# Gated delta rule: a root moved to GpSimd, one more round of lag, and two units' block merging taken together

## The chip, the cores and the metric

The kernel runs on one core of one Trainium2 chip. Its time is the device time of one execution in microseconds (us). It has five queues that run side by side: TensorE (PE; PEld is its weight load), VectorE (DVE), ScalarE (ACT), GpSimd (POOL), and the sync queue (SP), which here issues every DMA. Each queue is strictly in order; the queues wait for one another with semaphores.

## The reference, cut to what matters

The reference is a decoder of four layers on 16 sequences of 128 tokens and width 256, that is eleven more stages behind the one that is changed. The change is in the first stage, the gated delta rule:

```python
q, k, v = (silu(causal_conv4(x @ W)) for W in (Wq, Wk, Wv))      # 16 heads of 128
alpha, beta = sigmoid(x @ Wa + ba), sigmoid(x @ Wb + bb)
for each token:  S = alpha * S - beta * (S k - v) k^T ;  o = S q
o = (o - mean) * rsqrt(var + 1e-5) * ln_g + ln_b
out = (o * sigmoid(x @ Wg)) @ Wo
```

The kernel does the token loop of one sequence in closed form: with N the strictly lower, decayed 128x128 matrix of beta k k^T, it needs the inverse of (1 + N), applied to v, and then a second masked matrix applied to that.

## The kernel before

`Delta` (lines 320 to 832) does 64 units, one head of four sequences each, tile 128x512. `order()` (L452) writes out by hand a software pipeline of rounds: round t does the first half of unit a = t (projections k and q, convolutions, decay), the score matrices of unit t-1, and the second half of units v = t-LAG, w = t-LAG-1 and x = t-LAG-2 (projections v and gate, the rest of the inverse, the products, the norm, the output). PE, ACT and DVE all follow this one list of steps. In it PE's line L310 is a projection, L502 the scores, L518 and L527 and L530 the merging of 32x32 blocks (steps x32 and y32), L537 and L543 that of 64x64 blocks (x64, y64), L557 step w, L564 step o, L571 the turned o, L580 the output (acc), L550 the turned v.

The inverse of (1 + N) is made in two parts. The 32x32 blocks on the diagonal are inverted by GpSimd, for a batch of up to eight units (128 blocks, one on each partition): a first instruction (L826) and then 30 dependent pairs (L830, L831), and a turned copy (L832). The blocks reach it through DRAM: SP writes each unit's N (L380), reads a batch into `NB` (L387), writes the inverses out (`blocks_out`, L399) and reads them back by unit into `T` and `TT` (`blocks_in`, L409 and L412, seven DMAs a unit). Then x32, y32, x64 and y64 join the blocks: each is a handful of small matmuls into PSUM bank 7 and a copy by ACT (L647, L653, L654, L657, L660), one waiting for the other.

SP's queue is written by `load()` (L344): in iteration t it loads two weights for the unit t+4 once PE has done q of unit t, three weights for the second half, `blocks_out` and `blocks_in` where due, and then the N of unit t-1. There is one buffer `NB`, so the load of batch m waits for the inversion of batch m-1 (L385).

The norm of o (step o) is DVE's: four statistics (L222), four aggregates (L225) and then eleven small instructions on 128x4 for the inverse root (L196 to L214: a shift, a subtraction, three Newton steps) and one for the mean (L784). ACT applies it (step on, L678, four instructions) and only then may PE write bank 4 again: `room[4] = self.on.at(u + 1)`, which step s0 waits for. The rows of a group of four sequences are normed in steps stats, scale and turn, in every 16th round.

Of the kernel before, what the change touches and what calls it, by code (L numbers as in the profile page):

```python
# [11 lines left out]
ALU = mybir.AluOpType  # L12
# [3 lines left out]
NB = 16  # L16
T = 128
# [48 lines left out]
class Core:  # L66
# [4 lines left out]
    def __init__(self, nc, ctx, ins, out):  # L71
# [12 lines left out]
        self.rsq = self.at("rsq", [128, 16], F32)  # L84
        self.free0 = self.low
# [60 lines left out]
    def start_vector(self, dve, own):  # L146
        dve.memset(self.ones[:, :], 1.0)
        dve.wait_ge(self.dma_const, 48)
        dve.tensor_copy(self.identb[:, :], self.ident[:, :])
        dve.tensor_copy(self.neg[:, :], self.negf[:, :]).then_inc(*self.const.up)  # L150
# [51 lines left out]
    def rsqrt_rest(self, dve, own, w):  # L202
# [12 lines left out]
        return o  # L215

# [103 lines left out]
class Delta(Stage):  # L320
# [6 lines left out]
    U, LAG, RING = 64, 12, 14  # L327
    BATCHES = (4, 4) + (8,) * 6 + (4, 4)

    def weights(self):  # L330
# [4 lines left out]
        self.id32 = c.f32("did", 32, 32)  # L335
# [8 lines left out]
    def load(self, sp):  # L344
# [9 lines left out]
        sp.dma_start(self.id32[:, :, :], i["c_ident"][0:32, 0:32].unsqueeze(0).broadcast_to([128, 32, 32])).then_inc(small, 16)  # L354
        for t in range(-4, self.U + self.LAG):
# [15 lines left out]
            if 0 <= v - 1 < self.U:  # L371
                self.blocks_in(sp, v - 1)
            if 0 <= n < self.U:
# [7 lines left out]
                if n == self.first[m] + self.BATCHES[m] - 1:  # L381
                    so_far = sum(self.BATCHES[i] for i in range(m % 2, m + 1, 2))
                    sp.wait_ge(self.n_sem[m % 2], 64 * so_far)
                    if m:
                        sp.wait_ge(*self.sub.at(m))  # L385
                    P = 16 * self.BATCHES[m]
                    sp.dma_start(self.NB[0:P, :, :], self.Nd[m % 2].rearrange("u b k s t -> (u b k) s t")[0:P]).then_inc(self.nb_sem[m % 2], 16)  # L387
# [14 lines left out]
    def blocks_in(self, sp, v):  # L402
# [4 lines left out]
        for k in range(4):  # L407
            of = self.TTd[m % 2, v - self.first[m], :, k, :, :].rearrange("b c t -> c b t")
            sp.dma_start(g4(self.TT[v % 4][blk(k, 32), :])[:, :, blk(k, 32)], of).then_inc(self.t_sem[v % 4], 16)  # L409
        for k in range(3):  # L410
            of = self.Td[m % 2, v - self.first[m], :, k, :, :].rearrange("b t c -> t b c")
            sp.dma_start(self.T[v % 4][blk(k, 32), :, blk(k % 2, 32)], of).then_inc(self.t_sem[v % 4], 16)  # L412

    def buffers(self):
# [13 lines left out]
        self.TT, self.T, self.X = c.sets(4, "dTT", 512), c.sets(4, "dT", 4, 64), c.sets(2, "dX", 4, 64)  # L428
        self.NB, self.TB, self.TTB, self.tmp = c.f32("dNB", 32, 32), c.f32("dTB", 32, 32), c.f32("dTTB", 32, 32), c.f32("dtmp", 256)
# [13 lines left out]
        self.sc, self.vt, self.x32, self.y32, self.x64, self.y64 = t("score", 2 * U), t("v_turned", U), t("x32", U), t("y32", U), t("x64", U), t("y64", U)  # L443
        self.wm, self.o, self.ot, self.accd = t("w", U), t("o", U), t("ot", U), t("acc", U)
        self.ck, self.cq, self.cv, self.hk, self.hq, self.hv = s("k0", U), s("q0", U), s("v0", U), s("k_tanh", U), s("q_tanh", U), s("v_tanh", U)
        self.vk, self.xc32, self.yc32, self.xc64, self.yc64 = s("v", U), s("x32", U), s("y32", U), s("x64", U), s("y64", U)
        self.wc, self.on, self.os, self.gt, self.ex = s("w", U), s("o", U), s("o_turned", U), s("gate", U), s("exp", U)
        self.dk, self.dq, self.dv, self.sk, self.sq, self.sv = v("k", U), v("q", U), v("v", U), v("k_silu", U), v("q_silu", U), v("v_silu", U)
        self.nr, self.rs, self.go, self.summed = v("scores", 2 * U), v("o", U), v("gated", U), v("summed", 4)
        self.sub = p("inverses", len(self.BATCHES))  # L450

    def order(self):  # L452


        for t in range(self.U + self.LAG + 5):
# [4 lines left out]
            for step, u in every:  # L460
                if 0 <= u < self.U and (step not in ("close", "stats", "scale", "turn") or u % 16 == 15) and (step, u) != ("turn", self.U - 1):
                    yield step, u, u % self.RING, u // 16, u % 16

    def tensor(self, pe):
        c, bank, room = self.c, self.c.bank, self.c.room
        pe.wait_ge(self.dma[0], 176)
# [16 lines left out]
        for step, u, r, g, h in self.order():  # L483
# [28 lines left out]
            elif step == "x32":  # L512
                pe.wait_ge(*room[7])
                pe.wait_ge(self.dma[11 + u % 4], 112 * (u // 4 + 1))
                for b in range(4):
                    for k in range(2):
                        lo, hi = blk(2 * k, 32), blk(2 * k + 1, 32)
                        t = pe.matmul(bank(7)[hi, blk(b, 32)], self.NT[r][lo, 128 * b + 64 * k + 32:128 * b + 64 * k + 64],  # L518
                                      self.T[u % 4][lo, b, 0:32], start=True, stop=True, tile_position=(64 * k, 64 * k + 32))
                t.then_inc(*self.x32.up)  # L520
            elif step == "y32":
                pe.wait_ge(*self.xc32.at(u + 1))
                TT = g4(self.TT[u % 4][:, :])
                for b in range(4):
                    for k in range(2):
                        lo, hi = blk(2 * k, 32), blk(2 * k + 1, 32)
                        pe.matmul(bank(7)[lo, 128 + 32 * b:160 + 32 * b], self.X[s][hi, b, 0:32], TT[hi, b, hi], start=True, stop=True,  # L527
                                  tile_position=(64 * k + 32, 64 * k))
                    lo, hi = blk(0, 32), blk(1, 32)
                    t = pe.matmul(bank(7)[hi, 256 + 32 * b:288 + 32 * b], TT[hi, b, hi], self.X[s][hi, b, 0:32], start=True, stop=True,  # L530
                                  tile_position=(32, 32))
                t.then_inc(*self.y32.up)
            elif step == "x64":
                pe.wait_ge(*self.yc32.at(u + 1))
                lo, hi = blk(0, 64), blk(1, 64)
                for b in range(4):
                    t = pe.matmul(bank(7)[hi, blk(b, 64)], self.NT[r][lo, 128 * b + 64:128 * b + 128], self.T[u % 4][lo, b, :], start=True, stop=True)  # L537
                t.then_inc(*self.x64.up)
            elif step == "y64":
                pe.wait_ge(*self.xc64.at(u + 1))  # L540
                lo, hi, TT = blk(0, 64), blk(1, 64), g4(self.TT[u % 4][:, :])
                for b in range(4):
                    t = pe.matmul(bank(7)[lo, 256 + 64 * b:320 + 64 * b], self.X[s][hi, b, :], TT[hi, b, hi], start=True, stop=True)  # L543
                t.then_inc(*self.y64.up)
                room[7] = self.yc64.at(u + 1)
# [3131 lines left out]
```

## Time and profile before

| what | value |
|---|---|
| median of 3 runs | 3936.02 us (3934.26 to 3938.75) |
| the profiled execution | 3935.08 us, of which its span 3933.3 us |
| PE, DVE, ACT, POOL busy, whole span | 86%, 76%, 49%, 29% |
| the Delta stage | from 0 to about 1180 us |
| its rounds with both halves, 178 to 995 us | PE busy 793.7 of 817.0 us, DVE 736.3, ACT 519.6, POOL 261.6; granted clock 1.00 |
| its start, 0 to 178 us | PE busy 122.7 us, clock 0.89 |
| its end, 995 to 1180 us | PE busy 161.2 of 185.0 us, clock 0.94 |

A line of the timeline gives start, duration (from the start of the first to the end of the last instruction of a run of equal ones), engine, line, operation, tiles written and read, shapes and count; in brackets the idle time of the engine before it and what ended it. Matmuls overlap, so the time that a group takes of PE is the distance to the start of the next group, not its duration.

### The profile page before, as it was taken

What the parts mean: (1) busy time and instruction counts of PE and PEld (TensorE: products, weight loads), DVE (VectorE), ACT (ScalarE), POOL (GpSimd) and SP (SyncE); (2) the same over time, 40 slices, a digit from 0 to 9 for tenths busy, and PEclk for the clock granted to TensorE, in tenths of its full rate; (3) what the DMA queues carried; (4) which work ended last, traced back from release to release, by engine and by line L of the source; (5) the groups of instructions that cost most, each with busy time, mean ns of one, the idle gap of its engine ahead of it and who ended that gap; (6) DMA issues with size and microseconds to landing.
All of it is one profiled execution on the core that took longest, in us unless ns stands there. A gap on an engine that the chain in (4) does not pass through costs nothing.

```text
span 3933.3 us, 63955 instructions
## 1 busy us (share of the span) xinstructions
PE 3367.4 (86%) x22787; PEld 2145.2 (55%) x22802; DVE 2988.6 (76%) x6462; ACT 1945.5 (49%) x4750; POOL 1135.5 (29%) x1162
## 2 busy tenths in 40 slices
PE   7799999999886295888999978889999999997775
PEld 3366666665554243664556655565655656564444
DVE  7799988989656866554367767768988898986668
ACT  4466666666553142331144425436656655563455
POOL 1533033206401200000011122015655555554110
PEclk9899999999998598898999989899999999998887
DMA  2222222222211000001000000302222222222000
GB/s 71 61 71 56 68 63 68 58 63 62 51 34 47 13 23 24 2 2 63 1 22 1 1 33 2 123 6 89 78 70 76 70 75 76 70 75 77 1 1 22
DMA packets 240233, 183.98 MB, mean 47 GB/s; under 512 B 117744, under 2 KB 216432, under 8 KB 239024
## 3 DMA queue, kind: packets, MB, share of 16 engines
q1 hardware_dynamic: 239920, 179.90, 15.5%
q8 instruction: 185, 3.03, 0.3%
q14 instruction: 128, 1.05, 0.1%
HBM read 164.61 MB, written 15.20 MB: 46 GB/s over the span
## 4 chain that ended last, share of the span: by engine, by line
PE 59%; DVE 28%; issue 5%; ACT 5%; POOL 2%; SPq 1%; DMA 1%; DVEq 0%; ACTq 0%; POOLq 0%
PE ps L310 21%; PE ps L3273 5%; PE ps L2908 4%; PE ps L3261 3%; PE ps L502 2%; PE ps L2953 2%; DVE hMX L3026 2%; PE ps L2695 1%; DVE macc L3413 1%; PE ps L580 1%; PE ps L1972 1%; PE ps L3252 1%; PE ps L2914 1%; PE ps L2171 1%; PE ps L316 1%
## 5 line engine op out<-in xcount | busy, mean ns | idle before, releaser
L310 PE MATMUL ps<-xT,min 128*128 128x512 f32 (+1 forms) x1072 | 499.3, 610 | 30.2 <-DVE macc L3413 29.8
L3413 DVE SCALAR_TENSOR_TENSOR macc<-ps,mcw,macc 128x508 f32<-128x508 f32 (+2 forms) x408 | 302.2, 741 | 77.8 <-ACT macc L3340 68.1
L3495 POOL TENSOR_TENSOR mSQ<-mSQ,mtn 128x512 f32<-128x512 f32 x128 | 243.1, 1900 | 353.3 <-ACT mtn L3365 353.3
L310 PEld LDWEIGHTS ps<-xT,min 128*128 128x128 f32 (+1 forms) x1072 | 190.8, 190 | 249.2 <-issue 202.9
L3488 POOL TENSOR_TENSOR mE<-mE,mCB 128x1024 f32<-128x1024 f32 x128 | 302.1, 2360 | 44.4 <-DVE mE L3423 26.3
L3423 DVE TENSOR_TENSOR_SCAN mE<-mE,mid 128x1024 f32<-128x1024 f32 x128 | 297.3, 2322 | 0.0
L3273 PE MATMUL ps<-mwo,macc 128*128 128x256 f32 x1024 | 243.1, 380 | 5.4 <-DVE macc L3430 5.3
L3026 DVE TENSOR_REDUCE hMX<-ps 128x2 f32<-128x512 f32 x256 | 165.4, 687 | 104.1 <-PE ps L2914 104.1
L3361 ACT ACTIVATE mtn<-ps,mcol 128x64 f32<-128x64 f32 x1024 | 222.9, 334 | 2.8 <-PE ps L3252 2.8
L826 POOL TENSOR_TENSOR dTB<-did,dNB 128x1024 f32<-128x1024 f32 (+1 forms) x10 | 29.1, 2908 | 664.1 <-DMA dNB<-d_N 598.7
L2993 ACT ACTIVATE hE<-ps 128x512 f32<-128x512 f32 x256 | 138.9, 594 | 153.0 <-PE ps L2908 153.0
L2914 PE MATMUL ps<-hKE,hXE 32*128 32x256 f32 x1024 | 170.5, 457 | 37.8 <-issue 15.1
L3273 PEld LDWEIGHTS ps<-mwo,macc 128*128 128x128 f32 x1024 | 184.7, 190 | 28.5 <-DVE macc L3430 8.5
L2908 PE MATMUL ps<-hXE,hKE 32*128 32x256 f32 x1024 | 156.6, 423 | 49.5 <-DVE hMX L3026 40.2
L2360 POOL TENSOR_TENSOR lP<-lP,lm 128x512 f32<-128x512 f32 x64 | 66.8, 1044 | 452.2 <-DVE lm L2333 452.2
L732 DVE SCALAR_TENSOR_TENSOR dav<-ps,dsmall,dav 128x508 f32<-128x508 f32 (+2 forms) x192 | 142.3, 741 | 47.0 <-ACT dav L603 42.5
L831 POOL TENSOR_TENSOR dTB<-dTB,dtmp 128x30 f32<-128x30 f32 (+11 forms) x300 | 169.6, 565 | 23.5
L732 DVE SCALAR_TENSOR_TENSOR daq<-ps,dsmall,daq 128x508 f32<-128x508 f32 (+2 forms) x192 | 142.5, 742 | 42.6 <-ACT daq L603 37.2
L732 DVE SCALAR_TENSOR_TENSOR dak<-ps,dsmall,dak 128x508 f32<-128x508 f32 (+2 forms) x192 | 142.2, 741 | 25.1 <-ACT dak L603 20.5
L830 POOL TENSOR_TENSOR dtmp<-dNB,dTB 128x30 f32<-128x30 f32 (+11 forms) x300 | 154.0, 513 | 23.5
L502 PE MATMUL ps<-dKQ 128*128 128x256 f32 x512 | 137.7, 396 | 24.6 <-ACT dO L678 17.0
L2264 ACT ACTIVATE lP<-ps,lm 128x128 f32<-128x128 f32 x256 | 90.6, 366 | 129.9 <-DVE lm L2327 129.9
(594 smaller groups left out, 8281.0 us busy)
## 6 DMA issues: line engine op xcount, KB each, us to landing
mE<-m_decay SPq DMA_DIRECT2D x128, 512.0 KB, 3.7
dwk<-in_L_attn_Wk SPq DMA_DIRECT2D x64, 128.0 KB, 2.3
dwq<-in_L_attn_Wq SPq DMA_DIRECT2D x64, 128.0 KB, 2.3
dwv<-in_L_attn_Wv SPq DMA_DIRECT2D x64, 128.0 KB, 2.4
dwg<-in_L_attn_Wg SPq DMA_DIRECT2D x64, 128.0 KB, 2.4
dwo<-in_L_attn_Wo SPq DMA_DIRECT2D x64, 128.0 KB, 2.7
min<-in_m_in SPq DMA_DIRECT2D x2, 4096.0 KB, 17.1
d_N<-dNT SPq DMA_DIRECT2D x256, 16.0 KB, 1.5
```

Of the source, the lines that this page charges most:

```text
L310: t = pe.matmul(out, w[:, j, :], self.c.xT[:, j, blk(g, 512)], start=j == 0, stop=j == 1)
L502: t = pe.matmul(bank(4 + i)[:, blk(j, 256)], self.KQ[s][:, 2 * i + j, 0, :], self.KQ[s][:, 2 * i + j, :, :], start=True, stop=True)
L732: x = dve.scalar_tensor_tensor(out=acc[:, :, 3 - j:T], in0=p[:, :, 0:T - 3 + j], scalar=small[:, 4 * k + j:4 * k + j + 1], in1=acc[:, :, 3 ...
L2908: m = pe.matmul(self.c.bank(n)[:, blk(h, 256)], self.KE[x][r, e, blk(h)], self.XE[x][r, e, :], start=True, stop=True)
L2914: m = pe.matmul(self.c.bank(n)[:, blk(1 - h, 256)], self.XE[t % 4][r, h, blk(e)], self.KE[t % 4][r, h, :], start=True, stop=True)
L3026: dve.tensor_reduce(self.MX[y][:, k // 2, r:r + 32:16], bank(n).rearrange("p (e n) -> p e n", e=2), AX.X, ALU.max, negate=True).then_inc(* ...
L3273: t = pe.matmul(bank(to + j // 2)[:, blk(j % 2, 256)], self.acc[s][:, blk(j)], self.wo[:, i, :], start=i == 0 and j % 2 == 0, stop=i == 31 ...
L3361: x = act.activation(self.tn[s][:, h], bank(6)[:, h], ACT.Copy, scale=self.col[:, 4 * g + j, 2 * i + e:2 * i + e + 1])
L3413: x = dve.scalar_tensor_tensor(out=acc[:, :, 3 - j:T], in0=p[:, :, 0:T - 3 + j], scalar=self.cw[:, i, j:j + 1], in1=acc[:, :, 3 - j:T], op ...
L3423: dve.tensor_tensor_scan(E, E, self.id8[:, :, :].rearrange("p b t -> p (b t)"), 0.0, ALU.mult, ALU.add).then_inc(*self.de.up)
L3488: pool.tensor_tensor(E, E, bc(self.CB[g % 2][:, :, :].rearrange("p b t -> p (b t)"), 2), ALU.mult).then_inc(*self.em.up)
L3495: pool.tensor_tensor(self.SQ[g % 2][:, :], self.SQ[g % 2][:, :], self.tn[s][:, :], ALU.add).then_inc(*self.sqa.up)
```

## The change

Five things are changed in the stage.

1. The inverse root and the negated mean of step o go to GpSimd: DVE stops after the four aggregates and signals, GpSimd does four instructions on 128x4 (a product by -1, an addition, a power of -0.5, a product). The group's root in step stats goes there too (two instructions).
2. GpSimd's inversion is cut into parts (three of ten pairs each; the last batch into four), placed in the same rounds as the roots: in round t GpSimd does first the root of unit w, then the part that is due.
3. LAG is 13 instead of 12, the ring of N and its companion has 15 instead of 14 places, and the batches are (4, 4) and seven of 8, where they were (4, 4), six of 8, (4, 4).
4. There are two buffers `NB`; the load of batch m waits for the inversion of batch m-2. The first instruction of an inversion no longer reads an identity `did` (its DMA is gone) but is a product by -1 and a memset of the diagonal.
5. The steps x32, y32, x64 and y64 are done in every second round, for units u and u+1 together; the number of matmuls is the same, the copies of ACT are half as many and twice as wide. `blocks_in` is issued for both units in one iteration of SP, every second iteration.

```diff
-    U, LAG, RING = 64, 12, 14
-    BATCHES = (4, 4) + (8,) * 6 + (4, 4)
+    U, LAG, RING = 64, 13, 15
+    BATCHES = (4, 4) + (8,) * 7
...
-        sp.dma_start(self.id32[:, :, :], i["c_ident"][0:32, 0:32].unsqueeze(0).broadcast_to([128, 32, 32])).then_inc(small, 16)
...
-            if 0 <= v - 1 < self.U:
+            if 0 <= v - 1 < self.U and v % 2:
                 self.blocks_in(sp, v - 1)
+                self.blocks_in(sp, v)
...
-                    if m:
-                        sp.wait_ge(*self.sub.at(m))
+                    if m >= 2:
+                        sp.wait_ge(*self.sub.at(m - 1))
...
+                if step in ("x32", "y32", "x64", "y64") and u % 2:
+                    continue
...
             elif step == "x32":
                 pe.wait_ge(*room[7])
-                pe.wait_ge(self.dma[11 + u % 4], 112 * (u // 4 + 1))
-                for b in range(4):
-                    for k in range(2):
+                T = self.T[u // 2 % 2]
+                for z in range(2):
+                    pe.wait_ge(self.dma[11 + (u + z) % 4], 112 * ((u + z) // 4 + 1))
+                    N = self.NT[(u + z) % self.RING]
+                    for b in range(4):
+                        for k in range(2):
...
             elif step == "o":
-                o = c.moments(dve, own, [(p[:, blk(j)], 0) for j in range(4)], st, sw, 1e-5 / 128)
+                for j in range(4):
+                    o = own(dve.bn_stats(st[:, j, 0:6], p[:, blk(j)]))
                 dve.wait_ge(own.sem, o)
-                dve.scalar_tensor_tensor(out=st[:, :, 0:1].rearrange("p a b -> p (a b)"), in0=st[:, :, 6:7].rearrange("p a b -> p (a b)"),
-                                         scalar=-1.0, in1=sw[:, 0:4], op0=ALU.mult, op1=ALU.mult).then_inc(*self.rs.up)
+                for j in range(4):
+                    x = dve.bn_aggr(st[:, j, 6:8], st[:, j, 0:6])
+                x.then_inc(*self.var.up)
...
     def gpsimd(self, pool, own):
+        for t in range(self.U + self.LAG + 5):
+            w, x = t - self.LAG - 1, t - self.LAG - 3
+            if 0 <= w < self.U:
+                st, sw = self.s8[w % 2], self.sw[w % 2]
+                pool.wait_ge(*self.var.at(w + 1))
+                pool.tensor_scalar(flat(st[:, :, 0:1]), flat(st[:, :, 6:7]), -1.0, 1.0, ALU.mult, ALU.mult)
+                then(c.root_pool(pool, own, sw[:, 0:4], flat(st[:, :, 7:8]), 1e-5 / 128, sw[:, 4:8]))
+                pool.tensor_tensor(flat(st[:, :, 0:1]), flat(st[:, :, 0:1]), sw[:, 0:4], ALU.mult).then_inc(*self.rs.up)
+            if 0 <= x < self.U and x % 16 == 15:
+                pool.wait_ge(*self.xvar.at(x // 16 + 1))
+                c.root_pool(pool, own, c.rsq[:, 0:4], flat(c.st[:, :, 7:8]), 1e-5, c.pv).then_inc(*self.xrs.up)
+            for m, n in enumerate(self.BATCHES):
+                end = self.first[m] + n
+                rounds = {0: (4, 4, 4), 1: (8, 8, 14), len(self.BATCHES) - 1: (end, end + 1, end + 2, end + 3)}.get(m, (end, end + 1, end + 2))
+                for part, due in enumerate(rounds):
+                    if due == t:
+                        self.invert(pool, then, m, part, len(rounds))
...
+    def root_pool(self, pool, own, out, var, eps, tmp):
+        if eps:
+            o = own(pool.tensor_scalar(tmp, var, eps, 1.0, ALU.add, ALU.mult))
+            pool.wait_ge(own.sem, o)
+        return pool.tensor_tensor(out, tmp, self.half, ALU.pow)
...
-            then(pool.tensor_tensor(TB, self.id32[0:P], NB.rearrange("p s t -> p t s"), ALU.subtract))
-            for s in range(1, 31):
+            then(pool.tensor_scalar(TB, NB.rearrange("p s t -> p t s"), -1.0, 1.0, ALU.mult, ALU.mult))
+            then(pool.memset(TB.rearrange("p t c -> p (t c)")[:, 0::33], 1.0))
+        for s in range(1 + 30 * part // parts, 1 + 30 * (part + 1) // parts):
```

## Rows read from the trace of the kernel before

**Rows 1.** Timeline, PE, one round without GpSimd work (start us, us, group).

```profile
309.76 1.13 PE L502 MATMUL ps<-dKQ 128*128 128x256 f32 x4
...
314.30 0.67 PE L537 MATMUL ps<-dT,dNT 64*64 64x64 f32 x8
314.90 0.66 PE L571 MATMUL ps<-ident,dO 128*128 128x128 f32 x4
...
319.25 1.89 PE L580 MATMUL ps<-dwo,dGO 128*128 128x256 f32 x8
320.97 1.88 PE L310 MATMUL ps<-xT,dwk 128*128 128x512 f32 x4
322.78 0.44 PE L518 MATMUL ps<-dT,dNT 32*32 32x32 f32 x16
323.15 0.66 PE L550 MATMUL ps<-ident,dav 128*128 128x128 f32 x4
323.65 1.88 PE L310 MATMUL ps<-xT,dwq 128*128 128x512 f32 x4
...
325.89 1.13 PE L502 MATMUL ps<-dKQ 128*128 128x256 f32 x4
```

**Rows 2.** Timeline, ACT, the same round, up to s0.

```profile
322.89 0.78 ACT L603 ACTIVATE dak<-ps,dsmall 128x512 f32<-128x512 f32 x1 [2.30 <-PE ps L310]
323.57 0.26 ACT L647 COPY dX<-ps 128x128 f32<-128x128 f32 x1
...
324.34 1.50 ACT L678 ACTIVATE dO<-ps,dst,dsw 128x128 f32<-128x128 f32 x4
```

**Rows 3.** Timeline, DVE, the same round: the last product of the scores.

```profile
314.22 0.41 DVE L775 TENSOR_TENSOR dRT<-ps,dE 128x256 f32<-128x256 f32 x1
```

**Rows 4.** Waits of PE, 178 to 1100 us: total, times, longest.

```profile
PE ps L502 <- ACT dO L678: 17.0, 19, 2.1
PE ps L571 <- DVE dRT L775: 5.0, 4, 1.5
PE ps L537 <- ACT dT L654: 4.2, 3, 2.2
...
PE ps L518 <- DMA dT<-d_T: 3.1, 2, 1.6
```

**Rows 5.** Timeline, SP: start of a batch-closing iteration, and that batch's hand-over.

```profile
608.51 0.39 SPq L361 DMA_DIRECT2D dwk<-in_L_attn_Wk  x1
...
664.84 0.34 SPq L399 DMA_DIRECT2D d_T<-dTB  x1
...
668.81 1.75 SPq L409 DMA_DIRECT2D dTT<-d_TT  x4
```

**Rows 6.** Timeline, POOL: the inversion of that batch, start and after ten pairs.

```profile
622.01 2.90 POOL L826 TENSOR_TENSOR dTB<-did,dNB 128x1024 f32<-128x1024 f32 x1 [90.61 <-DMA dNB<-d_N]
...
636.84 0.57 POOL L830 TENSOR_TENSOR dtmp<-dNB,dTB 128x220 f32<-128x220 f32 x1
```

**Rows 7.** Groups of POOL by form, a later stage's root (busy us, mean ns | idle).

```profile
L2885 POOL TENSOR_TENSOR rsq<-hpw 128x4 f32<-128x4 f32 x8 | 8.2, 1020 | 0.7
L2883 POOL TENSOR_SCALAR hpw<-st 128x4 f32<-128x4 f32 x8 | 1.6, 196 | 106.2 <-DVE st L2873 106.2
```

**Rows 8.** Timeline, PE: the stage's first matmuls, and the first merging.

```profile
15.11 8.86 PE L473 MATMUL ps<-xT,dab 128*32 128x512 f32 x32 [2.97 <-DMA did<-in_c_ident]
...
142.59 0.64 PE L518 MATMUL ps<-dT,dNT 32*32 32x32 f32 x16 [21.01 <-DMA dT<-d_T]
```

**Rows 9.** Timeline, SP: the load for the second inversion, the first one's results out.

```profile
123.30 0.45 SPq L387 DMA_DIRECT2D dNB<-d_N  x1
...
133.81 0.47 SPq L399 DMA_DIRECT2D d_T<-dTB  x1
```

**Rows 10.** Timeline, PE: one round of the stage's end.

```profile
1102.04 0.44 PE L518 MATMUL ps<-dT,dNT 32*32 32x32 f32 x16
...
1113.08 0.44 PE L518 MATMUL ps<-dT,dNT 32*32 32x32 f32 x16
```

More of the change, by code:

```diff
@@ L147, in start_vector @@
         dve.memset(self.ones[:, :], 1.0)
+        dve.memset(self.half, -0.5)
         dve.wait_ge(self.dma_const, 48)
@@ L520, in tensor @@
                 t.then_inc(*self.x32.up)
             elif step == "y32":
[L522 to L531, printed above, removed]
+                pe.wait_ge(*self.xc32.at(u // 2 + 1))
@@ new lines, in tensor @@
+                for z in range(2):
+                    TT = g4(self.TT[u // 2 % 2][:, z, :])
+                    for b in range(4):
+                        for k in range(2):
+                            lo, hi = blk(2 * k, 32), blk(2 * k + 1, 32)
+                            pe.matmul(bank(7)[lo, blk(4 * z + b, 32)], self.X[hi, z, b, 0:32], TT[hi, b, hi], start=True, stop=True,
+                                      tile_position=(64 * k + 32, 64 * k))
+                        lo, hi = blk(0, 32), blk(1, 32)
+                        t = pe.matmul(bank(7)[hi, blk(8 + 4 * z + b, 32)], TT[hi, b, hi], self.X[hi, z, b, 0:32], start=True, stop=True,
+                                      tile_position=(32, 32))
@@ L538, in tensor @@
                 t.then_inc(*self.x64.up)
             elif step == "y64":
[L540 to L543, printed above, removed]
+                pe.wait_ge(*self.xc64.at(u // 2 + 1))
+                lo, hi = blk(0, 64), blk(1, 64)
+                for z in range(2):
+                    for b in range(4):
+                        t = pe.matmul(bank(7)[lo, blk(4 * z + b, 64)], self.X[hi, z, b, :], g4(self.TT[u // 2 % 2][:, z, :])[hi, b, hi],
+                                      start=True, stop=True)
@@ L655, in scalar @@
+                act.activation(self.T[u // 2 % 2][32:64, :, :, 0:32].rearrange("p z b n -> p (z b) n"), p[32:64, 1, :, :], ACT.Copy,
+                               scale=-1.0).then_inc(*self.yc32.up)
             elif step == "x64":
-                act.wait_ge(*self.x64.at(u + 1))
-                act.copy(self.X[s][64:128, :, :], bank(7)[64:128, 0:256].rearrange("p (b n) -> p b n", b=4)).then_inc(*self.xc64.up)
+                act.wait_ge(*self.x64.at(u // 2 + 1))
+                act.copy(self.X[64:128, :, :, :].rearrange("p z b n -> p (z b) n"),
+                         bank(7)[64:128, :].rearrange("p (b n) -> p b n", b=8)).then_inc(*self.xc64.up)
@@ L818, in gpsimd, with invert @@
         e.then_inc(*self.blank.up)
-        pool.wait_ge(self.dma[0], 176)
-        for m, n in enumerate(self.BATCHES):
-            P = 16 * n
-            NB, TB, tmp = self.NB[0:P], self.TB[0:P], self.tmp[0:P]
+        pool.wait_ge(self.dma[0], 160)
+        pool.wait_ge(*c.const.at(1))
+        for t in range(self.U + self.LAG + 5):
[15 more added lines that the diff above has]
+                        self.invert(pool, then, m, part, len(rounds))
+    def invert(self, pool, then, m, part, parts):
+        P = 16 * self.BATCHES[m]
+        NB, TB, tmp = self.NB[m % 2][0:P], self.TB[0:P], self.tmp[0:P]
+        if part == 0:
             pool.wait_ge(self.nb_sem[m % 2], 16 * (m // 2 + 1))
```

96 lines of the change are left out of this document (55 added, 41 removed).

## The prediction, made before the changed kernel was run

> **What bounds the kernel now.** I read the views in this order: the page, for the stage's place; the timeline of PE, ACT and DVE in a quiet round; PE's waits; then SP and GpSimd. After PE's first 178 us come 49 rounds with both halves. One without GpSimd work runs from one s0 to the next in 325.89 - 309.76 = 16.13 us, and PE hardly pauses in it [rows 1]. So PE sets the pace, and DVE's instructions cost nothing there by themselves. But one chain of other engines ends at the same instant: after projection k (PE until 322.78) ACT does the convolution of k, the copy of x32, one of V, and then the normed o, from 324.34 to 325.84 [rows 2]; s0 starts 0.05 us later [rows 1]. What delays the root delays this chain. From 178 to 1100 us PE waited 17.0 us for it (19 times), 5.0 us for the products of the scores, 4.2 us for block copies in the stage's end and 3.1 us for blocks [rows 4], 29.3 us in all. These waits are what can be won in the full rounds. The other places are the start (PE idle 2.97 us for `did`, later 21.01 us for the first blocks) [rows 8] and the number of rounds.
>
> **Start and first blocks.** `did` is the last DMA that PE awaits at 15.11; without it the weights and the turned x are there: -2.9 us, the idle time shown [rows 8]. The first inversion was over at 123.30, when the load of the second was let go, but its results left only at 133.81, because SP stood in front of that load [rows 9]. With two buffers SP is free. The results leave at 123.3 - 2.9 + 2.6 (five weight loads, as SP's iteration at 608.51 has) = 123.0. From that issue to x32 it was 142.59 - 133.81 = 8.8 us [rows 8, 9]; now seven more DMAs are issued, 1.75 us for four [rows 5], so 3.1 for seven: 134.9. Against 142.59 that is -7.7, and I take -7 for both steps together, as the merge of two units lasts longer.
>
> **Lag.** One more round of lag turns one full round (16.13) into an early one, which falls into PE's idle 21.01 us, and a late one. Late rounds take 1113.08 - 1102.04 = 11.04 us [rows 10]; I take 10.8 (below). -16.1 + 10.8 = -5.3.
>
> **Two units merged at once.** The matmuls are the same. PE's projection before x32 lasts 322.78 - 320.97 = 1.81 us, the output group before a like one 320.97 - 319.25 = 1.72 [rows 1]: 0.09 us for going into small tiles. I count the same for coming out. Four steps less in two rounds save 4 x 0.18 = 0.7 us. Against it, a round without merging has nothing to fill PE while it waits. (a) From the end of k, PE has the turn of V (0.50) and q (1.72), 2.2 us; ACT has 325.84 - 322.78 = 3.06 less the x32 copy's 0.28, plus 0.05 for the semaphore, 2.83 [rows 1, 2]: 0.6 us wait. (b) The turned o waits for the last product, over at 314.63, that is 4.87 after s0 [rows 3]; without x64 PE is there at 314.30 - 309.76 - 0.09 = 4.45: 0.4 us [rows 1]. In the merging round PE is the later one, no wait. A pair: 32.26 - 0.05 (s0's present wait) - 0.7 + 0.6 + 0.4 = 32.5, or +0.14 a round, 49 rounds: +6.9 us. The bounds: if both waits vanish -17, if the 0.7 is not saved +24.
> Late rounds have no k, q and s0. There the fewer and earlier steps of ACT and the earlier root give some of the 0.3 us waits back; I take -0.27 for 13 rounds, -3.5 (0 to -6).
>
> **Root on GpSimd.** A product 0.20, an addition 0.20, a wait, a power 1.02, a wait, a product 0.20 [rows 7], with four semaphore steps of some 0.07: 1.9 us. It starts at the end of the aggregates as DVE's twelve small instructions did, and those end in time in a quiet round (s0 has no wait over 0.05). So in quiet rounds it is worth nothing. In rounds with an inversion the waits of 17.0 and 5.0 go, and those of 4.2 and 3.1 by the earlier root and the longer lag: -29.3 [rows 4]. What comes instead has three terms.
> (i) GpSimd is in order, so the root stands behind a part. A batch took 664.84 - 622.01 = 42.8 us, the first ten pairs 14.8 [rows 5, 6], the other two parts about 15.5 and 12.5. Part and root make 16.7 or more against a round of 16.1 to 16.3. Also the part starts late. From the start of SP's iteration to the inversion were 622.01 - 608.51 = 13.5 us [rows 5, 6], and in these (even) rounds SP now issues a second unit's blocks ahead of the N: 16.6, or 16.1 after s0. Part 0 ends at 16.1 + 14.4 = 30.5 (the new first instruction reads one input instead of two and has no row: I take 0.4 less than 2.90, bounds 0 and half of it), the root at 32.4; ACT wants it at 31.0: 1.4 late. Part 1 and its root end 16.9 later, at 49.3, where s0 of that round bears 48.1: 1.2 late. 2.6 us at most, 0.5 if GpSimd, no longer held up by DVE's small steps, is 1 us quicker in each part. I take 1.5, for the six batches in full rounds: +9.
> (ii) DVE's other instructions on SBUF are still slowed by GpSimd, and the products come later by it: 2 of the old 5.0 us stay, +2.
> (iii) The waits behind a queue are few: on GpSimd nothing but parts and roots, on ACT everything from o on, which is (i).
>
> **Hand-over of a batch.** Its results now leave in an even round, and both units' blocks must land before the x32 of the next. SP's iteration starts with q's end, 0.5 us ahead of s0; 2.6 for the weights, 8.8 + 3.1 as above: 14.0 us after s0. PE gets to the second unit's blocks at 13.02 (k's end in [rows 1]) - 2 x 0.69 (no x64, y64) + 0.4 + 0.3 = 12.4. So PE waits 1.5 us, seven times: +10.5 (0 to +16).
>
> **The last batch.** It was (4, 4) and is 8 units now, and it falls into late rounds. Its x32 stands five rounds behind its last scores. After those scores (4.9 after s0) the inversion starts 8 us later at the latest, 6 at best; 42.8 for the parts, four roots of 1.9 between them, 0.6 of waiting, then 8.8 + 3.1 for the DMAs: 70 us. PE has, from the scores to that x32, 5 us to the end of its round and four late rounds, one with the turn of x: 55. It stands still for 14.7 us (10 to 18), and nothing in order can pass it.
>
> **Sum.** -7 - 5.3 + 6.9 - 3.5 - 29.3 + 9 + 2 + 10.5 + 14.7 = -2.0. From the profiled execution's own 3935.1 us (span 3933.3 and 1.8 around it) that is 3933.1; the median of the runs lies 0.9 above it: 3934. The later stages stay as they are.
>
> The Trainium skill, in "GPSIMD Engine Reference", section "Performance pitfalls for Q7 kernels", says that reading SBUF with a step over 8 bytes costs half as much again for each element. The new first instruction reads `NB` with a step of 32 numbers, so by that rule it keeps most of its time. The row has 2.90 us for the old one with the same step and a second input [rows 6]; which of the two makes it long no row tells. By the rule the 0.4 us in each of six batches would not come, and the sum would be 3936.
>
> **Rivals.**
> A. The pauses do not come: parts and roots are shorter than a round, the hand-over lands in time, the last batch is done in its five rounds. For it: two thirds of GpSimd's time in the stage is idle, and its inversions are measured under DVE's load. Then 9, 10.5 and most of 14.7 fall away: 3934 - 31 = 3903; half of it, 3918.
> B. Slower: GpSimd becomes the bound while a batch is in it. A part of 15.5 and a root of 1.9, with the power held up by DVE, last 17.4 or more. Every root of the three rounds then comes late for ACT, beyond the 1.0 us of slack there, and s0 waits about 2 us three times for six batches: 36 instead of 9. 3961, from the point where part and root exceed 17 us. Against it: the third part is short and lets GpSimd catch up.
> C. Slower: pairs cost more than I count, +0.5 a round, since each wait in the round without merging adds to the next: +18, 3952. Against it: one chain ends there at a time.
> D. It doesn't do what it says: the old waits come from something else than the root's small steps (the groups' sums). Then 10 of the 29.3 stay: 3944. Against it: 19 of the waits name ACT's normed o [rows 4].
>
> **Chances.** My forecast, with its mixed neighbours from 3926 to 3944, 45%; A 27%, B 10%, C 10%, D 8%. The forecast's own range is 3922 to 3946, the range for eight in ten 3906 to 3952. A measurement tells no change below 0.2%, 7.9 us, here 3928 to 3944. Faster: all of A and a fifth of the forecast, 36%; slower: B, C and some of D and the forecast, 26%; between them 38%.
>
> **What would show it.** In the trace after: the first merging near 135 us; quiet rounds in pairs of about 15.7 and 16.8; PE waits for ACT's o in every second quiet round; waits of 1 to 2 us for blocks at each batch; a pause near 15 us ahead of unit 56's x32; a root of 1.9 us from aggregates to signal. Rounds of equal length, or no pause at unit 56, would make it wrong.

## The result, and the profile after

The change makes the kernel a little slower. The median of 17 runs is 3945.81 us (3940.34 to 3959.41), that of 17 runs of the kernel before on the same chip 3938.01 us; the ratio is 1.0020, 95% interval 1.0013 to 1.0026, or 5 to 10 us. The forecast was 3934 (-2 us in the profiled execution), with a range of 3922 to 3946.

Here s0(u) is the start of unit u's first scores matmul, the start of a round; acc(63) is the last output group of the stage. "Window" is s0(13) to s0(62), 49 rounds; "tail" is s0(62) to acc(63). "Three stages" are Latent, Channels and Scan together, which the change does not touch. All are from one profiled execution each.

| kernel | s0(13) | window | tail | acc(63) | three stages | span |
|---|---|---|---|---|---|---|
| before | 178.1 | 817.1 | 179.2 | 1174.3 | 1613.0 | 3933.3 |
| after | 155.6 | 832.2 | 191.8 | 1179.6 | 1626.6 | 3952.6 |

The start brought what was expected (155), then 15 us are lost in the window and 12.6 in the tail. First PE, two quiet rounds of the changed kernel, to be held against [rows 1]:

```profile
430.44 1.13 PE L515 MATMUL ps<-dKQ 128*128 128x256 f32 x4 [0.60 <-ACT dO L702]
...
435.36 0.65 PE L592 MATMUL ps<-ident,dO 128*128 128x128 f32 x4 [0.33 <-DVE dRT L799]
...
442.48 0.69 PE L534 MATMUL ps<-dT,dNT 32*32 32x32 f32 x32
...
446.04 1.13 PE L515 MATMUL ps<-dKQ 128*128 128x256 f32 x4
...
450.57 1.14 PE L555 MATMUL ps<-dT,dNT 64*64 64x64 f32 x16
...
462.81 0.70 PE L515 MATMUL ps<-dKQ 128*128 128x256 f32 x2 [0.59 <-ACT dO L702]
```

From s0 to s0 the rounds last 15.60 and 16.77 us, 16.19 on average against 16.13 before. The two waits of 0.6 and 0.3 us are in the round of the program without merging; that round begins with projection k, so they stand on either side of an s0. So quiet rounds are as forecast. The loss must be in the others. These are PE's waits in the window; before it had only 3.1 us for dT [rows 4]:

```profile
PE ps L515 <- ACT dO L702: 23.2, 28, 1.9
PE ps L534 <- DMA dT<-d_T: 15.9, 7, 2.9
PE ps L592 <- DVE dRT L799: 7.9, 22, 0.8
```

One hand-over of a batch, SP first (this answers to [rows 5]), then PE, then the granted clock in the stretches before and after PE's pause (start:end, length, busy of PE, PE's weight loads, DVE, ACT, POOL, clock, DMA share, GB/s):

```profile
393.26 0.39 SPq L368 DMA_DIRECT2D dwk<-in_L_attn_Wk  x1
...
395.88 0.34 SPq L407 DMA_DIRECT2D d_T<-dTB  x1
...
400.21 1.74 SPq L417 DMA_DIRECT2D dTT<-d_TT  x4
402.00 1.38 SPq L420 DMA_DIRECT2D dT<-d_T  x3
403.42 1.86 SPq L417 DMA_DIRECT2D dTT<-d_TT  x4
405.32 2.29 SPq L420 DMA_DIRECT2D dT<-d_T  x3
```

```profile
405.88 0.44 PE L534 MATMUL ps<-dT,dNT 32*32 32x32 f32 x16
408.87 0.64 PE L534 MATMUL ps<-dT,dNT 32*32 32x32 f32 x16 [2.56 <-DMA dT<-d_T]
409.44 1.11 PE L571 MATMUL ps<-ident,dav 128*128 128x128 f32 x4
410.35 2.75 PE L319 MATMUL ps<-xT,dwq 128*128 128x512 f32 x4
```

```profile
393.80:406.30 12.50, 12.14 (x66) 7.86 (x66) 9.86 (x23) 6.51 (x13) 1.62 (x4) 1.00 0.49 152
408.90:413.66 4.76, 4.76 (x72) 2.86 (x72) 0.19 (x1) 2.88 (x7) 0.00 (x0) 0.66 0.07 10
```

The first unit's blocks are in time, the second's are not. PE can go on with them 15.0 us after s0 (393.8), forecast 14.0; it was there at 406.3, 12.5 after s0, forecast 12.4. And there is a second cost that the forecast had at nothing: after the pause the granted clock falls to the lower level (1.2 GHz, clock 0.66 over 4.8 us), so projection q takes 2.75 us until its end instead of 1.88. The round lasts 19.84 us instead of 15.61. The six hand-over rounds of the window last 4.73, 2.06, 4.23, 3.55, 4.62 and 4.63 us more than a quiet one, 23.8 in all where 9 were forecast. PE's waits for the second unit's blocks in them are 2.92, 1.88, 2.56, 1.73, 2.82 and 2.76 us, 14.7 in all; behind each but the second stands a stretch of 3.4 us at 1.2 GHz, and these rounds are 1.7 to 1.9 us longer than their wait. The seventh hand-over of the window, behind s0(59), has no wait: there SP has no more weights of k and q to load.

The second place is the round with an inversion part: DVE (aggregates), GpSimd, ACT, PE.

```profile
352.77 0.38 DVE L810 BATCH_NORM_AGGREGATE dst<-dst 128x2 f32<-128x6 f32 x4
```

```profile
342.08 2.01 POOL L883 TENSOR_SCALAR dTB<-dNB 128x1024 f32<-128x1024 f32 x1 [3.70 <-DMA dNB<-d_N]
...
355.66 0.60 POOL L889 TENSOR_TENSOR dTB<-dTB,dtmp 128x210 f32<-128x210 f32 x1
356.35 0.20 POOL L862 TENSOR_SCALAR dst<-dst 128x4 f32<-128x4 f32 x1
356.61 0.20 POOL L222 TENSOR_SCALAR dsw<-dst 128x4 f32<-128x4 f32 x1
356.89 1.03 POOL L224 TENSOR_TENSOR dsw<-dsw,st 128x4 f32<-128x4 f32 x1
358.00 0.20 POOL L864 TENSOR_TENSOR dst<-dst,dsw 128x4 f32<-128x4 f32 x1
```

```profile
358.24 1.50 ACT L702 ACTIVATE dO<-ps,dst,dsw 128x128 f32<-128x128 f32 x4 [1.25 <-POOL dst L864]
```

```profile
359.79 1.13 PE L515 MATMUL ps<-dKQ 128*128 128x256 f32 x4 [1.95 <-ACT dO L702]
360.76 1.78 PE L578 MATMUL ps<-dV,dTT 128*128 128x128 f32 x8
```

The moments are ready at 353.15, but GpSimd is in the part until 356.3; root and signal take 1.9 us as forecast, and s0 waits 1.95 us, 1.36 more than in a quiet round (forecast 1.4). Behind it the clock is again low (w 1.78 us instead of 1.05), but the next round is no longer for it: it lasts 17.27 us here and 17.23 and 17.21 us behind s0(33) and s0(41), where the clock stays at 1.00. These rounds cost 16.3 us over the window, 11 were forecast. In the tail one pause stands out, forecast 14.7 us, measured 11.0 + 2.4:

```profile
1072.73 0.64 PE L534 MATMUL ps<-dT,dNT 32*32 32x32 f32 x16 [10.98 <-DMA dT<-d_T]
1075.73 0.64 PE L534 MATMUL ps<-dT,dNT 32*32 32x32 f32 x16 [2.36 <-DMA dT<-d_T]
```

The start of the stage, for [rows 8]. The forecast of 134.9 was for the blocks of both units. The first unit's merging starts at 135.90, the second's at 139.10, 4.2 us late: the results left SP at 127.06, not at 123.0.

```profile
135.90 0.64 PE L534 MATMUL ps<-dT,dNT 32*32 32x32 f32 x16 [8.34 <-DMA dT<-d_T]
139.10 0.64 PE L534 MATMUL ps<-dT,dNT 32*32 32x32 f32 x16 [2.56 <-DMA dT<-d_T]
```

### The profile page after: what moved, and what is told of

It reads as the page before. It is cut to its first block and busy times, and to the rows that moved or that the text cites. A ratio compares the mean times of both kernels' runs of the same rounds, so it can differ in the third digit from the quotient of the medians.

```text
span 3952.6 us, 63063 instructions
## 1 busy us (share of the span) xinstructions
PE 3364.9 (85%) x22787; PEld 2155.7 (55%) x22802; DVE 2804.1 (71%) x5583; ACT 1917.7 (49%) x4558; POOL 1207.2 (31%) x1369
## 5 line engine op out<-in xcount | busy, mean ns | idle before, releaser
L2973 PE MATMUL ps<-hKE,hXE 32*128 32x256 f32 x1024 | 174.0, 464 | 37.8 <-issue 15.1
L862 POOL TENSOR_SCALAR dst<-dst 128x4 f32<-128x4 f32 x64 | 13.0, 203 | 556.8 <-DVE dst L810 555.0
L889 POOL TENSOR_TENSOR dTB<-dTB,dtmp 128x30 f32<-128x30 f32 (+11 forms) x270 | 156.5, 580 | 21.2
L2967 PEld LDWEIGHTS ps<-hXE,hKE 32*128 32x128 f32 x1024 | 103.2, 201 | 89.9 <-issue 50.3
```

The lines of the kernel that those rows point to most:

```text
L889: then(pool.tensor_tensor(low, low, piece, ALU.subtract))
L2967: m = pe.matmul(self.c.bank(n)[:, blk(h, 256)], self.KE[x][r, e, blk(h)], self.XE[x][r, e, :], start=True, stop=True)
L2973: m = pe.matmul(self.c.bank(n)[:, blk(1 - h, 256)], self.XE[t % 4][r, h, blk(e)], self.KE[t % 4][r, h, :], start=True, stop=True)
```

## The experiments

Theory 1: a batch's hand-over is late by SP's order, and its pause lowers the clock. Theory 2: the root is late because GpSimd's parts start late, behind SP's loads for a pair, and this too comes from merging in pairs. Rival: GpSimd with parts and roots doesn't fit into the rounds, or DMA queues are the bound, whatever the order.

| kernel | median us | ratio to before, 95% | window | tail | acc(63) | three stages |
|---|---|---|---|---|---|---|
| e1 results first | 3940.4 | 0.9996 (0.9985 to 1.0007) | 818.8 | 193.2 | 1167.7 | 1622.9 |
| e2 last batch (4, 4) | 3944.6 | 1.0007 (0.9997 to 1.0017) | 830.4 | 187.1 | 1173.8 | 1622.9 |
| e3 first part short | 3939.0 | 0.9996 (0.9986 to 1.0005) | 819.5 | 193.4 | 1170.5 | 1622.9 |
| e4 root on DVE | 3944.0 | 1.0012 (1.0002 to 1.0022) | 834.3 | 186.3 | 1177.9 | 1622.9 |
| e5 N first | 3981.1 | 1.0123 (1.0110 to 1.0137) | 856.7 | 197.9 | 1212.2 | 1622.9 |
| e6 before, lag 13 | 3911.5 | 0.9944 (0.9930 to 0.9958) | 812.3 | 182.6 | 1150.0 | 1612.4 |
| e7 single merging | 3910.4 | 0.9941 (0.9928 to 0.9955) | 796.4 | 185.3 | 1135.2 | 1623.1 |
| f1 combined | 3954.6 | 1.0056 (1.0043 to 1.0070) | 841.0 | 182.6 | 1179.1 | 1623.1 |
| a0 after again | 3947.0 | 1.0022 (1.0013 to 1.0032) | 836.0 | 191.8 | 1184.5 | 1622.9 |
| b0 before again | 3934.7 (one run) | - | 819.7 | 177.3 | 1174.8 | 1612.6 |
| e9 spread loads | 3935.5 | 0.9994 (0.9982 to 1.0005) | 821.9 | 192.2 | 1172.3 | 1622.9 |
| e10 spread, out early | 3909.7 | 0.9942 (0.9923 to 0.9960) | 797.6 | 192.2 | 1143.4 | 1622.8 |
| f2 single, last (4, 4) | 3898.6 | 0.9900 (0.9885 to 0.9915) | 795.1 | 177.2 | 1128.5 | 1623.0 |
| f5 = f2, closing roots on DVE | 3895.4 | 0.9896 (0.9879 to 0.9913) | 794.5 | 175.1 | 1123.2 | 1612.8 |
| e12 = e6, closing roots on GpSimd | 3913.2 (one run) | - | 805.2 | 182.0 | 1142.5 | 1623.2 |

**e1.**

```diff
+            for m in out:              # blocks_out without its own wait
+                self.blocks_out(sp, m)
             if 0 <= v < self.U:        # the loads of wv, wg and wo
...
-                if t == u0 + self.LAG - 1:
-                    self.blocks_out(sp, m)
+            for m in out:
+                sp.wait_ge(self.out_sem[m % 2], 32 * (m // 2 + 1))
```

> Edit: in the SP iteration of a hand-over the two DMAs that write a batch's results out are issued ahead of the five weight loads, and only their completion is waited for behind them. Theory 1 (the hand-over is late by SP's order, and its pause lowers the granted clock): blocks are loaded from 3.8 us after the round's s0 instead of 6.4, the 2.3 to 2.9 us waits of x32 for dT go in the six full rounds, and with them the 1.7 us at the lower clock; the hand-over rounds (19.2 to 20.3 us now) come down to about 16, some 24 us in all. Rival (the excess of these rounds is something else, DMA queues filled by the double load of blocks): the blocks still land about as late, the rounds stay over 18.5 us, 6 us or less in all. The pause at unit 56 stays in both.

The window fell by 13.4 us, about half. The hand-over rounds are 16.3 to 17.7 us, in between both expectations. The edit did less than its text says: the results go ahead of three weight loads, not five. In the round looked at above (s0 at 391.59 here) they leave 0.5 us after s0 and the blocks follow from 5.1 us, not 3.8, and the first four take 2.72 us to issue instead of 1.74:

```profile
392.10 0.34 SPq L409 DMA_DIRECT2D d_T<-dTB  x1
...
396.67 2.72 SPq L421 DMA_DIRECT2D dTT<-d_TT  x4
```

PE still waits 1.37 us for the second unit, and the clock stays at 1.00 behind it. The direction is the theory's; e10 tells whether the rest is too.

**e2.** `BATCHES = (4, 4) + (8,) * 6 + (4, 4)`, the ninth batch's results out at t == 64, the last inversion in rounds end+1 to end+3.

> Edit: the last batch of 8 is split into (4, 4) as before the change; the results of the first four leave in iteration 64 and the last four are inverted in rounds 65 to 67. Theory (the pause of 11 + 2.4 us ahead of unit 56's x32 is the wait for one inversion that starts only behind the last scores): x32(56) has no pause, the tail from the last s0 to the last acc falls from 191.8 us to about 180, and unit 60's x32 waits for nothing. Rival (GpSimd, in order with the roots, is then late for unit 60 instead): the pause moves to x32(60), and the tail gets at most 4 us shorter. The full rounds stay as they are in both.

The pause at unit 56 went, but the tail fell by 4.7 us only: the rival. In late rounds, 9.7 to 12.1 us long, a part of some 13 us delays a root, and ACT's copies for the merge stand behind o. ACT, then PE:

```profile
1072.11 1.51 ACT L702 ACTIVATE dO<-ps,dst,dsw 128x128 f32<-128x128 f32 x4 [4.52 <-POOL dst L864]
1073.50 0.74 ACT L675 ACTIVATE dTT<-ps 32x256 f32<-32x256 f32 x2
1074.26 0.38 ACT L676 ACTIVATE dT<-ps 32x256 f32<-32x256 f32 x1
```

```profile
1074.68 1.97 PE L555 MATMUL ps<-dT,dNT 64*64 64x64 f32 x16 [4.16 <-ACT dT L676]
```

**e3.** `cut = (1, 8, 18, 29, 31)`: steps of the four parts, in rounds end to end+3.

> Edit: the inversion of a full batch is cut into four uneven parts (steps 1 to 7, 8 to 17, 18 to 28, 29 and 30 with the turned copy) in rounds end to end+3 instead of three equal ones. Theory 2 (the root is late because the parts with it don't fit between two aggregates; the late root stops s0 and lowers the clock): roots start within 0.3 us of their aggregates, the rounds of part and root lose their excess of 0.8 to 1.8 us, 14 us of 16.3 in all. The results are ready 1 to 2 us after the start of the hand-over round, so its waits stay within 1 us of 2.5. Rival (GpSimd's work slows the DVE and ACT chain, whatever the order of root and part): the rounds with parts stay 1 us too long each, and there are more of them; no gain, or a loss by a later hand-over.

The window fell by 12.7 us, 14 expected. The round with part 0 went from 18.1 to 16.77 and the next from 17.3 to 16.04; the hand-over rounds stayed at 17.6 to 21.1. GpSimd's whole work fits, if the part that starts late is short enough to end ahead of the next root.

**e4.** DVE's step "o" is `c.moments(...)` and the last product again; GpSimd's loop issues parts only.

> Edit: everything of the change stays but the root of o's norm, which is DVE's twelve small steps again; GpSimd only inverts. What it tells: what the moved root alone is worth. Theory (of the forecast): the waits of before come back in rounds with an inversion (about 22 us for ACT's o and the products), the late roots' 16 us go, so the Delta stage gets 5 to 12 us longer. Rival: the old waits came mostly from the short lag and the single block buffer (blocks, copies), and the stage gets 5 us or more shorter with DVE's root.

The Delta stage ends 1.7 us earlier than in the change, between the two expectations: with pairs the moved root is worth 2.1 us in the window and costs 5.5 in the tail. The 2.1 us are not clear of noise: two profiles of the change itself differ by 3.8 us in the window (after and a0).

**e5.** In the iteration that ends a batch, `blocks_in` of the pair stands behind N and NB.

> Edit: only in the SP iteration that ends a batch, the four writes of N and the load of NB go ahead of the fourteen block loads of the pair, which the next round needs some 12 us later. Theory 2 (the root is late because the parts start late behind SP's block loads): NB is there 3 to 3.7 us earlier, part 0 ends before the aggregates of its round, and the excess of the part rounds falls by 12 to 16 us over six batches. The hand-over waits stay, since SP's iteration, not the inversion, places them. The pause ahead of unit 56's x32 gets 3 us shorter. Delta ends at about 1163. Rival (parts and roots do not fit into a round wherever they start): part 1's root stays late by about 1 us and at most 6 us go; the block loads behind N may come late instead.

My worst miss: 32.6 us more in the Delta stage. The late roots went, as expected. But the pair's blocks are wanted 12.4 us after the s0 with which SP's iteration begins, not a round later; I had taken the round wrong. PE paused twice for them, and the clock fell again (this round 21.56 us):

```profile
344.92 0.44 PE L538 MATMUL ps<-dT,dNT 32*32 32x32 f32 x16 [0.83 <-DMA dT<-d_T]
348.59 0.44 PE L538 MATMUL ps<-dT,dNT 32*32 32x32 f32 x16 [3.22 <-DMA dT<-d_T]
```

So the iteration that ends a batch can't have both in time: fourteen loads and the batch's N compete for the same 12 us of SP. This is what merging in pairs brings, and neither of the two orders within the iteration cures it; e9 and e10 spread the loads over two iterations.

**e6.** The kernel before with `LAG, RING = 13, 15`, two NB, and the first instruction without `did`.

> Edit: the kernel before with three parts of the change alone: lag 13 (ring 15), two NB buffers, the first instruction without did. Root on DVE, one inversion in one piece, merging unit by unit, batches (4, 4) at the end. By the forecast's steps: start and first blocks -7, lag -5.3, the waits for blocks and copies in the later rounds (4.2 + 3.1) gone, the waits for ACT's o of 17 us unchanged: Delta ends near 1156, the run at 3918 or so. Rival (the old waits for o come from the short lag, through the groups' sums and late blocks): it ends 10 us earlier still. Against both: if the lag is worth nothing, 1170.

Delta ended at 1150.0, 24.3 us earlier, forecast for these steps 19.6. From 178 to 1100 PE still waits 11.7 us for ACT's o (17 times) and 8.9 us for the products of the scores, 20.6 us where there were 22.0 [rows 4]: the lag doesn't remove them. In e7, with the root on GpSimd, 4.3 us are left.

**e7.** The x32 to y64 steps of before (one unit a round), with blocks loaded by `blocks_in(sp, v - 1)` in every iteration; all else as changed.

> Edit: the change with block merging undone: each unit is merged in its own round, blocks are loaded unit by unit in every SP iteration, root and parts stay. Theory: quiet rounds all last 16.1 (16.19 on average now, -3 over 49), the hand-over needs only seven DMAs behind the results, so its waits and the low clock behind them go (-24), N is written 3 us earlier and the late roots go down by 8 to 14, the last pause by 3; late rounds cost 1.5 more. Delta ends 35 us earlier, near 1145, and the merging is the part that made the change slow. Rival (pairs are not to blame, the late roots and hand-over come from GpSimd's order): Delta ends at 1165 or later.

Nearly all as expected. Delta ended 44.4 us earlier than with pairs (35 expected), 35.8 of it in the window. So merging in pairs, with all that it brings, is what made the change slow. Hand-over rounds are 16.12 us, and from s0(19) on no round of the window is over 17.1. From e6 to e7 (both kinds of root from DVE to GpSimd, the inversion in parts) the window gets 15.9 us shorter: without pairs the moved roots are worth what the forecast gave, or more (-22.0 + 9 + 2 = -11 for what e6 had not yet won). Not all of it is o's root: e12, which moves only the four closing roots, has a window 7.1 us shorter than e6's. With o's root on GpSimd they are worth nothing there (f2 795.1, f5 794.5). The pause at unit 56 stays (10.1 us).

**f1.** e5's order, the results out at the end of the iteration before, the last batch (4, 4) in six parts.

> The change with three repairs: N of a batch ahead of the block loads; the results of a batch written out at the end of the SP iteration before, their completion awaited ahead of the first block load; the last batch split into (4, 4) with the last inversion in six parts of five steps. Theory: late roots -14, hand-over -24, last pause -12: Delta ends near 1130 against 1179.6, the run 45 us under the change and 38 under the kernel before, at 3900. Rival (each repair uncovers the next wait, late roots in the late rounds above all): half of it, 3920.

It inherits e5's late blocks: the rounds that end a batch last 20.9 to 22.6 us. The other two repairs work: hand-over rounds 15.6, no pause at units 56 and 60. Expected 3900, measured 3954.6.

**a0 and b0.** The two kernels again.

> The changed kernel, unaltered. If the later stages' time is a matter of the execution, Channels, Latent and Scan may come out shorter this time (183, 397, 1033 us as in the profile of before); if it belongs to the kernel, they show 189, 398 and 1036 to 1039 again. The Delta stage ends at 1179.6 within 1 us in both.

> The kernel before, unaltered. As for the changed kernel: either Channels, Latent and Scan show 183, 397 and 1033 us again (the kernel's own), or lengths between these and 189, 398 and 1039 (by execution). Delta ends at 1174.3 within 1 us.

Latent, Channels and Scan take the same again in each: 1612.6 for before, 1622.9 for after. So this difference belongs to the kernel. The Delta stage is less steady than I said: a0's ended 4.9 us later than the first profile's, mostly for one hand-over (the round behind s0(27) 21.52 us instead of 19.84, the next 18.61 instead of 16.77).

**e9.**

```diff
-            if 0 <= v - 1 < self.U and v % 2:
+            if v % 2 and v - 1 in self.first:
                 self.blocks_in(sp, v - 1)
+            if 0 <= v < self.U and v not in self.first:
                 self.blocks_in(sp, v)
```

> Edit: pairs are still merged in every second round, but the blocks of a pair's first unit are loaded in the SP iteration before, those of the second in the one that held both; only a batch's first pair is still loaded together, behind the results. Theory: N goes out 3 us earlier than in the change without blocks coming late, part 0 starts 2.5 to 3 us earlier, and 11 to 14 of the 16 us of the part rounds go; the hand-over rounds stay at 19 to 20; Delta ends near 1166. Rival (the root is late for another reason): Delta ends within 4 us of 1179.6.

The root of the part round is in time (16.78 and 15.91 us where there were 18.12 and 17.27), the hand-over rounds are 17.6 to 21.1. Delta ended 7.3 us earlier, 14 expected: the window is 10.3 us shorter, but s0(13) came 2.7 us later, which the runs don't explain.

**e10.** e9, and `blocks_out` called at the end of the SP iteration `t == first + LAG - 2`, its completion awaited by the batch's first `blocks_in`.

> Edit: the spread loads, and the results of a batch written out at the end of the SP iteration before the one that loads its first pair, which waits only for their completion. Theory (late N and late hand-over are the whole excess of pairs in the full rounds): x32 has no wait at a batch's first pair, the six hand-over rounds last under 16 us, the window from s0(13) to s0(62) takes 800 us (832 in the change, 822 with spread loads), Delta ends near 1148. Rival (the block loads themselves come too late in a pair's round): hand-over rounds of 17 and more stay, and the window takes 812 or more.

The window is 797.6 us, 800 expected, and no wait for dT is left in it. The six hand-over rounds last 15.60 us each. This is the decisive run: with the pairs kept and only SP's order changed, the window is within 1.2 us of e7's without pairs. So late results and late N are the whole excess of pairs in the window; the tail stays at 192.2 us, against 185.3 in e7. The SP lines for the third full batch:

```profile
377.06 0.34 SPq L411 DMA_DIRECT2D d_T<-dTB  x1
...
383.76 1.80 SPq L422 DMA_DIRECT2D dTT<-d_TT  x4
...
388.93 1.38 SPq L425 DMA_DIRECT2D dT<-d_T  x3
```

```profile
393.84 0.69 PE L539 MATMUL ps<-dT,dNT 32*32 32x32 f32 x32
```

The last block loads start 7.1 us after s0 here (381.80), 11.5 us after it in the change (405.32 against 393.83); x32 does both units without a break.

**f2.** e7 with the last batch (4, 4), its last inversion in six parts of five steps.

> The change with merging undone (each unit in its own round) and the last batch as (4, 4), its last inversion in six parts. The run with merging undone had one pause of some 12 us ahead of unit 56's x32; theory: it goes, Delta ends near 1125 instead of 1135.2, and the run is at 3900, 33 us under the kernel before. Rival (late roots in the late rounds eat it): Delta ends at 1132 or later.

Nearly as expected: no pause at 56 or 60, tail 177.2 against 185.3, Delta ends at 1128.5, median 3898.6.

**f5 and e12.** In f5 `stats` is `c.moments(...)` on DVE again for the four closing norms; e12 adds only these four roots on GpSimd to e6.

> Edit: the kernel with single merging and a last batch of (4, 4), with the four roots of the closing norm of x (not those of o's norm) back on DVE. Theory 3 (moving these four roots is what shifts the later stages): Latent, Channels and Scan take 1613 us instead of 1623, Delta ends at 1128.5 within 2, the run is at 3889. Rival (something else in the change, or only where the stages fall): they take 1623 again and the run stays at 3899.

> Edit: the kernel before with lag 13 and two NB buffers, and with the four closing roots alone on GpSimd. Theory 3: Latent, Channels and Scan take 1623 us instead of 1612. Rival: they take 1612 to 1613 as in that kernel without them. Delta ends at 1150 within 2 in both.

In the later stages both came out by theory 3: moving four roots of 2 us each sets how long three later stages take in the profile. The rest was missed: Delta ended 5.3 us (f5) and 7.4 us (e12) earlier than I said. The stage Channels in b0, after and f5:

```profile
2335.10:2517.80 182.70, 150.05 (x1697) 93.48 (x1698) 130.43 (x280) 86.13 (x162) 33.77 (x66) 0.89 0.04 13
```

```profile
2342.40:2531.50 189.10, 156.58 (x1697) 96.34 (x1698) 130.61 (x280) 85.53 (x162) 33.56 (x66) 0.86 0.04 13
```

```profile
2284.40:2467.60 183.20, 149.80 (x1704) 93.31 (x1701) 130.90 (x281) 86.59 (x162) 33.10 (x65) 0.90 0.03 12
```

The same matmuls take PE 6.5 us more at a mean clock of 0.86 instead of 0.89. The first difference is near the end of Latent, 372.5 us behind its first matmul: 3.4 us at 1.2 GHz in all 13 profiles with the four roots on GpSimd and in none of the four without. f5 and f2 have the same PE pause of 2.09 us ahead of it. How the roots do it is not shown. f5's profiled execution took 3880.5 us, but its three others 3894.8 to 3896.4, so the gain is not there in each. The median is 3895.4 where theory 3 said 3889 and the rival 3899, and the ratios of f5 and f2 (0.9896 and 0.9900) don't differ beyond their intervals.

## Why the prediction was wrong

By place, the terms of the sum make -23.1 us up to s0(13), +5.4 in the window and +15.7 in the tail (of the waits of 29.3 us, 23.0 were in the window). Measured are -22.5, +15.1 and +12.6. So the miss of the Delta stage is in the window. There the waits of before were won in full (26.9 us over quiet rounds, 23.0 counted) and pairs cost less in quiet rounds; the hand-over and the late roots cost more.

- **Start, lag:** right in size. s0(13) came at 155.6 for 155; e6 brought 24.3 us for a forecast of 19.6. In part this is luck: both units' blocks were there 4.2 us later than forecast (139.10 for 134.9).
- **Two units merged at once, in quiet rounds:** the mechanism is right, with both named waits, the size too high: 0.06 us a round, 3 us in all, for +6.9 (the forecast's own sum of 32.5 makes 0.12 a round, not 0.14). But the forecast priced pairs as PE's matter. e7 puts their cost at 44.4 us of Delta, and e10, which keeps them and changes SP's order alone, gets 36.2 of these back.
- **Root on GpSimd:** the sum of -29.3, +9 and +2 holds with single merging (15.9 us, e6 to e7, the closing roots included) and not with pairs (2.1, e4). I had seen that part 0 starts 3 us late behind the pair's loads, and worked out 2.6 us for the two late roots of a batch. Then I took 1.5, as GpSimd might be quicker without DVE's small steps. The rounds with parts cost 16.3 us for six batches, 2.7 each: the working was right and the discount wrong, 5.3 us over the 11 forecast.
- **Hand-over of a batch:** the failed step. "So PE waits 1.5 us, seven times: +10.5": it is 23.8 us for six, and nothing for the seventh, 13.3 over the forecast; this alone turns -2 into a loss. The waits are 1.7 to 2.9 us, 14.7 in all. I priced fourteen loads by the issue time of seven more (3.1 us), and they took 1 us longer. And I took a pause for its own length: the other 9.1 us come behind the waits, 1.7 to 1.9 us at the lower clock in five of the six rounds.
- **The last batch:** right, 13.3 for 14.7. e2 and f2 show that (4, 4) with the last inversion in parts removes the pause; in e2, with larger parts, late roots take most of the gain, in f2, with six small ones and single merging, they don't.
- **"The later stages stay as they are":** wrong in the profiles, 10.3 us between b0 and a0 (13.6 between the first two), by the four closing roots (f5, e12). The profiles of a0 and b0 lie 14 us apart, the medians of the runs 8, and f5's unprofiled runs don't show the gain: how much of the 10 us is in the 7.8 between the medians is open.
- The rule of the Trainium skill that I weighed ("GPSIMD Engine Reference", "Performance pitfalls for Q7 kernels": a step over 8 bytes makes reads half as dear again) would have kept the first instruction near its 2.90 us [rows 6]. It takes 2.01 with the same step, 2.17 with the memset. The step stayed and the second input went, but the operation changed too, so no run here tells which of these made the old one dear.

The median of 3945.8 lies 0.2 us inside the forecast's own range, 3922 to 3946. That is luck: the hand-over and the late roots were priced 18.6 us too low, and other terms of the sum too high. None of the rivals is what happened. B had the right place (roots late by the parts), but with 36 us where 16.3 came; C had the right culprit and the wrong path.

## What to carry to other kernels

Merging work of two rounds into one also doubles the loads that one iteration of the loading queue must place by one deadline, if they are issued together; write out that queue's iteration against the earliest need before pricing the matmuls, and see whether the loads can be spread over two iterations (e10). Price a stall of the matrix engine with what the clock may take behind it: here 2.6 us cost 4.2. And once the engine that sets the pace has been freed, the order in which a queue issues can be worth more than the instructions moved: 34.6 us of the window from the change to e10, 15.9 for the roots from e6 to e7. With single merging, roots between parts and a last batch of (4, 4), f2 and f5 are 1.0% faster than the kernel before.

## What the runs showed of the hardware

- In a round that keeps PE busy, one pause of 1.4 us (e1) left the round 1.6 us longer, one of 2.6 us 4.2 longer. Behind five of the change's six hand-over pauses (1.73 to 2.92 us) the granted clock was at 1.2 GHz for 3.4 us and then back at 2.4 GHz; behind the sixth, of 1.88 us, it stayed at 2.4 GHz and the round was 2.1 us longer. So the length of the pause alone doesn't decide it.
- The granted clock of a stage can depend, repeatably, on small work in a stage that ended more than 1100 us before it: Channels takes 183 us in 4 of 4 profiles without the four closing roots on GpSimd, 189 us in all 13 with them, with PE's order of work the same. The three other runs of f5 took 14 to 16 us longer than its profiled one, so a run without the profiler may not show it.
